# A folded adapter kernel: five leading weight transfers, one product for the bias sums, one shared transpose

## The reference, cut to what matters

```
cond   = x @ W.T + b + 2.0 * (x @ A[slot]) @ B[slot]            # rank 16
base   = cond @ base_w.T + base_b
hidden = cond @ ffnA.T                                           # rank 64
logits = cond @ router_w.T                                       # 16 experts
combine = the two largest softmax weights, normalised, the others 0
out    = x + base + 0.5 * sum over e of combine[e] * hidden @ B[e].T
```

## Time and profile before

| what | value |
|---|---|
| median of three timed runs | 102.38 us (102.50, 101.35, 102.38) |
| profiled execution, its own time | 101.29 us |
| its span | 99.5 us |
| PE busy | 95.7 us of the span (96%) |
| DVE, ACT, POOL busy | 66.0, 41.5, 21.4 us |
| granted TensorE clock | 1.00 over the span |

### The profile page before, as it was taken

The page is one execution under the profiler, slowest core; times in us unless marked ns, Lnnn a source line. Parts: engine busy times, 40 slices in busy tenths (PEclk is TensorE's granted clock), DMA queues, the critical chain, the costliest instruction groups (busy, mean ns, idle before and its releaser), DMA issues.

```text
span 99.5 us, 1812 instructions
## 1 busy us (share of the span) xinstructions
PE 95.7 (96%) x572; PEld 87.1 (87%) x572; DVE 66.0 (66%) x184; ACT 41.5 (42%) x101; POOL 21.4 (21%) x34
## 2 busy tenths in 40 slices
PE   6899999999999999999999999999999999999990
PEld 6799999999999999998898799887788787888980
DVE  5669996997475885995997577257949274572101
ACT  1713536878787545754442510551434031040000
POOL 4100004325999965107022000000000000000000
PEclk9999999999999999999999999999999999999999
DMA  2999669999357777892593472616237082020311
GB/s 47 337 362 389 188 132 338 303 403 362 78 93 195 209 227 158 235 209 56 142 243 114 128 204 102 213 37 194 107 95 234 25 232 84 0 105 0 112 53 53
DMA packets 8443, 16.92 MB, mean 170 GB/s; under 512 B 1571, under 2 KB 4131, under 8 KB 8434
## 3 DMA queue, kind: packets, MB, share of 16 engines
q1 hardware_dynamic: 7762, 16.41, 55.2%
q10 hardware_dynamic: 640, 0.40, 1.3%
q0 software_dynamic: 32, 0.00, 0.0%
HBM read 13.28 MB, written 2.16 MB: 155 GB/s over the span
## 4 chain that ended last, share of the span: by engine, by line
PE 93%; DMA 3%; DVE 0%; ACT 0%; issue 0%
PE pair L825 90%; DMA w_raw_all<-w_cat 3%; PE pair L970 1%; PE pair L972 1%; PE pair L990 1%; DVE xn L819 0%; ACT w_hi_all L425 0%; PE pair L960 0%; PE pair L949 0%; PE pair L947 0%; PE pair L939 0%
## 5 line engine op out<-in xcount | busy, mean ns | idle before, releaser
L825 PE MATMUL pair<-e_hi,w_hi_all 128*128 128x512 f32 (+1 forms) x72 | 27.1, 376 | 0.0
L825 PE MATMUL pair<-e_hi,w_lo_all 128*128 128x512 f32 (+1 forms) x72 | 26.7, 370 | 0.0
L825 PE MATMUL pair<-e_lo,w_hi_all 128*128 128x512 f32 (+1 forms) x72 | 26.7, 370 | 0.0
L538 ACT ACTIVATE w_hi_all<-exp_raw_all 128x512 fp32r<-128x512 f32 x16 | 9.7, 629 | 15.9 <-DVE exp_raw_all L760 15.8
L825 PEld LDWEIGHTS pair<-e_hi,w_lo_all 128*128 128x128 f32 x72 | 13.6, 188 | 2.5
L825 PEld LDWEIGHTS pair<-e_hi,w_hi_all 128*128 128x128 f32 x72 | 13.6, 188 | 2.5
L825 PEld LDWEIGHTS pair<-e_lo,w_hi_all 128*128 128x128 f32 x72 | 13.6, 189 | 2.0
L767 DVE TENSOR_TENSOR w_lo_all<-exp_raw_all,w_hi_all 128x512 fp32r<-128x512 f32 x16 | 10.4, 689 | 4.5 <-ACT w_hi_all L538 4.0
L760 DVE TENSOR_TENSOR exp_raw_all<-w_raw_all 128x512 f32<-128x512 f32 x16 | 11.0, 725 | 0.9 <-DMA w_raw_all<-spill 0.9
L774 DVE TENSOR_TENSOR xn<-pair,xn 128x512 f32<-128x512 f32 x7 | 4.8, 691 | 8.6 <-PE pair L825 8.6
L825 PE MATMUL pair<-p_hi,x_hi 128*128 128x304 f32 x32 | 10.0, 311 | 0.0
(11 more groups left out here) (107 smaller groups left out, 161.5 us busy)
## 6 DMA issues: line engine op xcount, KB each, us to landing
w_raw_all<-spill SPq DMA_DIRECT2D x16, 256.0 KB, 4.0
xt_raw<-x_t SPq DMA_DIRECT2D x4, 512.0 KB, 7.0
exp_raw_all<-experts SPq DMA_DIRECT2D x4, 512.0 KB, 8.4
xn<-x_n SPq DMA_DIRECT2D x4, 512.0 KB, 5.4
out<-xn SPq DMA_DIRECT2D x7, 256.0 KB, 2.8
w_raw_all<-w_cat SPq DMA_DIRECT2D x2, 552.0 KB, 6.5
c_stack<-c_hi SPq DMA_DIRECT2D x7, 74.0 KB, 3.8
c_stack<-c_lo SPq DMA_DIRECT2D x7, 74.0 KB, 4.2
```

The lines of the kernel that those rows point to most:

```text
L538: nc.scalar.activation(gt_hi[:, t % 2, js, :], g[:, js, :], ACT.Copy).then_inc(gh_done, 1)
L825: return nc.tensor.matmul(out_ap, lhs, rhs, start=first, stop=last)
```

## The change

Block 0 comes in five transfers. ACT issues columns 0 to 127 alone, then `W_RIGHT`; SP issues columns 128 to 255 between its two transfers of the second factor. The bias sums of partitions 64 to 127 are moved down by ACT and added to those of 0 to 63 by DVE, so that the high parts (64 partitions) and the low parts (the other 64) stand in one tile and one product of ones sums both. The LoRA transpose of block 2 is no longer made alone, but rides in the routing transpose of block 0, which moves behind the first three matmuls of `x_other(2)`.

```diff
@@ SP
-            for n, cols in enumerate((W2_LEFT, W2_RIGHT)):
-                sp.dma_start(w_raw[:, 0, cols], w_cat[0, :, cols]).then_inc(in_w2_side[n], 16)
+            sp.dma_start(w_raw[:, 0, W2_LEFT], w_cat[0, :, W2_LEFT]).then_inc(in_w2_side[0], 16)
+            sp.dma_start(w_raw[:, 0, P:2 * P], w_cat[0, :, P:2 * P]).then_inc(in_w_second, 16)
+            sp.dma_start(w_raw[:, 0, W2_RIGHT], w_cat[0, :, W2_RIGHT]).then_inc(in_w2_side[1], 16)
@@ ACT
-            for n, cols in enumerate((W_LEFT, W_RIGHT)):
-                act.dma_start(w_raw[:, 0, cols], w_cat[0, :, cols]).then_inc(in_w_side[n], 16)
+            act.dma_start(w_raw[:, 0, 0:P], w_cat[0, :, 0:P]).then_inc(in_w_side[0], 16)
+            act.dma_start(w_raw[:, 0, W_RIGHT], w_cat[0, :, W_RIGHT]).then_inc(in_w_side[1], 16)
...
-            act.wait_ge(in_w_side[0], 16)
-            for cols in (slice(0, P), slice(P, 2 * P)):
+            for cols, loaded in ((slice(0, P), in_w_side[0]), (slice(P, 2 * P), in_w_second)):
+                act.wait_ge(loaded, 16)
...
             split_experts(0)
+            act.wait_ge(bias_step, KC)
+            nc.scalar.activation(bias_up[:, :], bias_part[P // 2:, :], ACT.Copy).then_inc(bias_moved, 1)
             act.wait_ge(pe_c, 1)
             nc.scalar.activation(c_hi[:, :], w2_cols(ps_c), ACT.Copy).then_inc(ch_done, 1)
-            act.wait_ge(bias_step, KC)
-            nc.scalar.activation(bp_hi[:, :], bias_part[:, :], ACT.Copy).then_inc(bph_done, 1)
+            act.wait_ge(bias_added, 1)
+            nc.scalar.activation(bp_split[0:P // 2, :], bias_up[:, :], ACT.Copy).then_inc(bph_done, 1)
...
-                if t in (3, 4):
-                    act.wait_ge(pe_ht, t - 1)
-                elif t >= 5:
+                if t == 3:
+                    act.wait_ge(pe_ht, 2)
+                elif t >= 4:
                     act.wait_ge(pe_rt, t - 3)
...
             routing_rows(0)
             exps(1)
-            lora_t_alone(2)
+            lora_t(2, ps_rt[T_H:P, :])
@@ DVE
             bias_part_of(1)
+            bias_part_of(2)
             folded_lo(0)
...
             folded_lo(3)
-            bias_part_of(2)
             bias_part_of(3)
+            dve.wait_ge(bias_moved, 1)
+            nc.vector.tensor_tensor(bias_up[:, :], bias_part[0:P // 2, :], bias_up[:, :],
+                                    ALU.add).then_inc(bias_added, 1)
             dve.wait_ge(ch_done, 1)
...
-            nc.vector.tensor_tensor(bp_lo[:, :], bias_part[:, :], bp_hi[:, :].bitcast(F32),
+            nc.vector.tensor_tensor(bp_split[P // 2:, :], bias_up[:, :], bp_split[0:P // 2, :].bitcast(F32),
                                     ALU.subtract).then_inc(bpl_done, 1)
@@ PE
-                x_side(t, out_cols, cols, bias_within=t == 0).then_inc(pe_x, 1)
+                x_side(t, out_cols, cols, within=t in (0, 2)).then_inc(pe_x, 1)
...
-                    if k == KC - 1 and bias_within:
+                    if k == KC - 1 and t == 0 and within:
                         bias()
+                    if k == 1 and t == 2 and within:
+                        routing_transpose(0)
...
-                halves(ps_b, BANK - W2H, W2H, ones[:, :], bp_hi[:, :], True, False)
-                halves(ps_b, BANK - W2H, W2H, ones[:, :], bp_lo[:, :], False, True).then_inc(pe_bias, 1)
+                halves(ps_b, BANK - W2H, W2H, ones[:, :], bp_split[:, :], True, True).then_inc(pe_bias, 1)
...
-                if 3 <= t + 2 < NT:
+                if t + 2 < NT:
                     cols = P
                     pe.wait_ge(ht_set, 2)
                     pe.wait_ge(hh_done, t + 3)
...
             x_first(2)
-            routing_transpose(0)
             lora_product(1)
             x_other(2)
-            lora_transpose(2)
             x_first(3)
```

More of the change, by code:

```diff
@@ L99, in adaln_ffn_kernel @@
         bias_part = sb("bias_part", [P, W2N])
-        bp_hi = sb("bp_hi", [P, W2N], F32R)
-        bp_lo = sb("bp_lo", [P, W2N], F32R)
+        bias_up = sb("bias_up", [P // 2, W2N])
+        bp_split = sb("bp_split", [P, W2N], F32R)
         bias_hi = sb("bias_hi", [FT, W2N], F32R)
@@ L182, in adaln_ffn_kernel @@
         in_w_next = sem("in_w_next")
+        in_w_second = sem("in_w_second")
         in_slots = sem("in_slots")
@@ L211, in adaln_ffn_kernel @@
         bias_step = sem("bias_step")
+        bias_moved = sem("bias_moved")
+        bias_added = sem("bias_added")
         bph_done = sem("bph_done")
@@ L910, in x_other, with x_side @@
                 out_cols, cols = other_half[t % 2]
-                x_side(t, out_cols, cols, bias_within=t == 0).then_inc(pe_x, 1)
-            def x_side(t, out_cols, cols, bias_within=False):
+                x_side(t, out_cols, cols, within=t in (0, 2)).then_inc(pe_x, 1)
+            def x_side(t, out_cols, cols, within=False):
                 par = t % 2
@@ L955, in lora_transpose @@
                 pe.wait_ge(ht_done, t)
-                if t >= 2:
-                    pe.wait_ge(ht_again_done, t - 1)
-                    pe.wait_ge(rt_done, t - 1)
                 nc.tensor.transpose(ps_ht, routed[:, t % 2, T_H:P], ident[:, :]).then_inc(pe_ht, 1)
```

## The result

The changed kernel takes 104.5 us in the median of six runs (102.95 to 105.14), the kernel before 102.18 beside it; the ratio is 1.014, between 1.008 and 1.021 with 95%. The forecast was 102.8 in a range of 101.0 to 103.3, so the time lies above the range.

What follows compares the result with a forecast made beforehand. PE bounds the kernel, working 95.7 of 99.5 us. The terms +0.50 - 0.27 + 0.10 + 0.08 - 0.11 + 0.15 = +0.45 us, on 102.38, gave 102.8 us, range 101.0 to 103.3.

Steps and rivals of the forecast that it cites:

- The start: First transfers, copies and casts before PE's first products: 0.2 us gained to 0.2 lost, taken as 0.
- The absorption: At the bias product, PE's earlier or later arrival changes nothing, as DVE's chain sets the time; the start counts 0.
- The clock rival: Bias stall drops TensorE to 1.2 GHz; over 2% slower, 105.0 us with block 1's 24 matmuls at that level; chance 0.03.
- The bias sums: At the ones product: two matmuls fewer gain 0.27 us; sum held by POOL, low half at 24.18, stall 0.50.
- The rival that had this chain in time: POOL doesn't hold the bias sum, or less; no bias stall, -0.30 us, so 101.0 or 102.1; chance 0.25.
- `x_first(1)`: Matmul behind the bias product, waiting for DVE's `first_low` at 25.0 to 25.2; 0 to 0.25 us lost, taken as 0.10.
- The overlap that was counted at 0.08: DVE's `bp_lo` output moves to partition 64, another quadrant, and is held for one overlap of 0.08 us, inside the bounds.
- The shared transpose: `routing_transpose(0)` waits for `lora_lo(2)`: 0 to 0.15 us lost, taken as 0.08; one transpose fewer gains 0.11.
- POOL and `x_first(4)`: POOL 0.68 us late, small subtraction held by DVE, `x_lo_part(4)` ends at 36.5; 0 to 0.35 us lost, taken as 0.15.
- The first product: PE's first matmul, at 4.25 before, can start no earlier than 4.07; 0 to 0.18 us gained.
- The rival that counted on it: The start's gain arrives too, with the bias chain in time: another 0.18 us, so 100.8 or 101.9; chance 0.07.

Runs made afterwards that it cites:

- f1: The changed kernel with SP waiting for the second factor's right half before issuing block 1 and all later transfers; 104.69 us, ratio 1.026.
- a1: The changed kernel with the four leading transfers of the kernel before, bias sum and shared transpose kept; 102.51 us, ratio 1.006.
- a2: The kernel before with the change's five transfers alone; 103.06 us, ratio 1.007.
- b1: The changed kernel with SP's second and third transfers exchanged, the second factor's right half before columns 128 to 255; 105.2 us, ratio 1.026.
- b0: The changed kernel again, unaltered, giving its second trace; 103.25 us, ratio 1.015 to the kernel before.
- b3: The changed kernel without ACT's scattered 3 KB probe transfer and SP's wait for it; 102.94 us, ratio 1.014.
- f3: The changed kernel a third time, unaltered, beside the one with four matmuls of zeros in PE's hole; 103.37 us, ratio 1.015.
- d1: a1 with POOL's `x_lo_part(2)` behind its wait for the bias's low half and its last expert quarter behind `x_lo_part(4)`; 102.04 us, ratio 1.002.

## Why the prediction was wrong, step by step

**The start: the step that failed.** It said that `W2_RIGHT` is issued one issue later, carries the same bytes in the same order, and that "PE wants them later than they come"; bounds 0.2 gained to 0.2 lost, taken as 0. Second on SP the right half landed at 4.0 to 4.4 in nine traces, third, with the large ones right behind it, at 5.6 to 6.1 in seven: against the 4.32 of the kernel before not one issue (0.5 us) later but 1.3 to 1.8. PE wants it behind six matmuls, 1.6 us after its first product even at the lower level, so at 5.65. One issue later alone would have stayed about within the bounds: with the large transfers held back (f1) it landed at 4.87, its cast started 0.21 later than before (4.90 against 4.69), and PE's seventh matmul followed without a wait. The rows that warned of it are in the trace of before, and the prediction doesn't use them: the third transfers of both queues there, issued at 1.65 us.

```profile
w_raw_all<-w_cat SPq DMA_DIRECT2D x1, 424.0 KB, 5.1
...
probe<-w_cat ACTq DMA_DIRECT2D x1, 3.0 KB, 5.3
```

A transfer of 3 KB that takes 5.3 us says that its own bytes aren't what counts. Taken as the worst case, these rows put the right half at up to 1.65 + 5.3 = 6.95 us, where one issue after 4.32 would be 4.8; it came at 5.98 and 6.10.

**The absorption failed with it.** "DVE's chain hangs on transfers and POOL, not on PE" is wrong: the earlier trace rows have DVE waiting for ACT's `p_hi` at 16.12, and `p_hi` waits for PE's fold. ACT and DVE of the second trace of the changed kernel:

```profile
16.73 0.67 ACT L459 ACTIVATE p_hi<-pair 128x592 fp32r<-128x592 f32 x1 [2.90 <-PE pair L837]
...
17.43 1.60 DVE L660 TENSOR_TENSOR p_lo<-pair,p_hi 128x592 fp32r<-128x592 f32 x2 [1.19 <-ACT p_hi L459]
```

In a1 they start at 15.46 and 16.16, so 1.27 us of PE's late start go through ACT and DVE to the bias product's low half (25.45 against 24.18), and the wait of 0.4 us stands there in full. Start and bias chain shift together, and nothing is absorbed. The 0.91 us of idle time ahead of that row was the sign that PE leads there.

**In time** the second trace's 1.31 us are the lateness of DVE's cast (4.69 to 6.00). On PE's side they look so: its first twelve matmuls take 7.52 - 4.03 = 3.49 us against 1.96 before, less the 0.22 of the earlier start. Over the dense 1.64 this is 1.85: a hole of 0.72 (5.65 to 6.37), 0.80 for six matmuls before it at the lower pitch, 0.33 for four after it, restarts and the wait for DVE's low part. The 0.80 is no loss of its own: at the upper pitch PE would have come to the hole that much earlier and stood the longer.

**The clock rival** (0.03) had the kind of cost right, work at the lower pitch, but not where and how it comes. It put a fall of the clock behind the bias stall, where no trace shows one. What happened is that TensorE stayed at the lower level in the start: in the first trace, a2 and b1 the pitch is 0.25 us to 9.4 to 10.0 us, which costs the first trace another 10.50 - 9.16 = 1.34. All three have the hole, but it is not enough to explain them: in b0 the level has risen when the hole ends, and b3 and f3, at the upper level before it, have weight loads of 0.19 us right behind it. As to the earlier trace rows, that window is 0.4 us of a column that shows 1.00 over the lower pitch as well: it was no evidence against.

**The bias sums** held: 1.48 us for the sum, 24.18, 24.33, as a1 shows. The rival that had this chain in time (0.25) was wrong, and d1 shows why it would have been right without POOL. The Trainium skill (VectorE: DVE Perf Modes, "Two Vector instructions with no wait between them") names a second SBUF read interface that is shared with GpSimd. The traces agree with it, and give the price: the sum takes 0.83 us alone and 1.48 beside POOL, the addition 0.77 and 1.14.

**`x_first(1)`** lost 0.21, not 0.10, in a1: it starts at 25.33 where the predicted slot is 25.12. That is within the bounds. The overlap that was counted at 0.08 is gone as predicted: DVE's small subtraction started at 23.41, 0.09 before the end of `bp_lo` at 23.50, and in a1 at 24.21, 0.03 after the end of the low half at 24.18.

**The shared transpose** lost 0.25, not 0.08, and beyond its bound of 0.15. The data were there at 31.42 (DVE's subtraction from 31.24 and 0.18), which with one release of 0.14 is 0.04 past the slot, as predicted. But PE's sequencer takes its six waits in four steps, which it passed at 31.45, 31.56, 31.66 and, with the weight load, 31.74; the matmul started at 31.77. From release to matmul this is 0.35 us, where one wait takes 0.14. I took the price of one step for a row of four.

**POOL and `x_first(4)`**: `x_lo_part(4)` ended at 36.62, predicted 36.5, but by another way: the small subtraction ran in 0.32 us, and the large one took 2.30 instead of 1.28. It cost nothing, since the slot had moved by the other losses to 36.81. In the table of a1: +0.04 start, +0.46 bias, -0.27, +0.21, +0.25, -0.11 = +0.58 us; its last matmul is 0.59 late. That this is near the predicted 0.45 is partly luck: 0.15 too much for `x_first(4)` stands against 0.11 and 0.17 too little for `x_first(1)` and the transpose.

**The first product** did come 0.23 earlier, more than the 0.18 allowed, because DVE's cast moved too (3.39 to 3.70). The rival that counted on it was right in that, and the late right half outweighs it nearly six times.

**Open.** Why the large transfers delay the one ahead of them in third place, by 0.7 to 1.2 us if f1's one trace is the measure, and not in second, where they stand right behind it in the kernel before (3.1 us). In the first trace half of the 16 DMA engines had done their part of the right half by 4.41 and the others ended at 5.5 to 6.1, with single packets of 1184 bytes taking 1.0 to 1.6 us. And why kernels with the same start differ between executions in how long PE stays at the lower level.

## What to carry to other kernels

Before a transfer is put in front of another, look up what each place of that queue costs in the trace that you have, a small transfer's row above all: if 3 KB take 5.3 us in third place, what you move there may take as long. Ask too what large transfers follow it: here they made the difference. A stall further on hides a late start only if the chain behind the stall doesn't begin with the late engine: follow it back to its first wait. Where an engine waits for a landing, work before the wait that runs slower costs nothing of its own. And read the clock by the distance between matmuls of one shape and by the weight loads beside it: a distance of 0.25 us can be the lower level or a wait.

## What the runs showed of the hardware

- The granted clock's column showed 1.00 over 5.4 us in which matmuls of 296 columns came 0.25 us apart instead of 0.137 (first trace). Weight loads of 128 columns took 0.33 us there and 0.19 at the upper level.
- 148 KB from the same source took 2.6 to 3.2 us in first or second place of SP's queue, 3.9 to 4.4 in third, and 3.2 in third with nothing behind it (f1). Holding back SP's large transfers also brought 3 KB on ACT's queue from 4.1 to 3.0 us.
- Of two instructions with two SBUF inputs on DVE and POOL, either can be the one held: DVE's sum 0.83 to 1.49, POOL's subtraction 1.28 to 2.32.
- Waits in a row before a matmul cost about 0.1 us each on PE's sequencer, even when only the first had anything to wait for (a1: 31.45, 31.56, 31.66).
